# A decoder layer on one core: the context's projection of the cross attention in three passes instead of a plain float32 matmul

## What is computed

```python
def _L0_xattn_ref(input1, input2, ...):          # input1 = layernorm(x), input2 = ctx_2048
    theta_x = einsum('ld,bdt->btl', theta_w, input2) + theta_b
    phi_x = einsum('ld,bdt->blt', phi_w, input1) + phi_b[:, None]
    scores = einsum('btl,bls->bts', theta_x, phi_x)
    p = softmax(scores, axis=-1)
    g_x = einsum('ld,bdt->btl', g_w, input1) + g_b
    t_x = einsum('bts,bsl->blt', p, g_x)
    h = relu((t_x - mu) * rsqrt(var + LN_EPS) * ln_gamma + ln_beta)   # mu, var over all of t_x of a batch
    w_t = einsum('ol,blt->bot', out_w, h) + out_b[None, :, None]
    return w_t + input2
```

## Time and profile before

| | |
|---|---|
| time, median of 3 runs | 2928.14 us (2927.73 to 2932.61) |
| profiled execution | 2930.81 us, its span 2929.1 us |
| mean granted TensorE clock | 0.982 |
| PE busy | 2793.4 us, 95% |
| DVE busy | 1236.7 us, 42% |
| ACT busy | 877.9 us, 30% |
| Pool busy | 838.8 us, 29% |

### The profile page before, as it was taken

One profiled execution on the slowest core, in us unless ns is written; L12 is line 12 of the kernel. 1 busy time (PEld: TensorE's weight loads), 2 busy tenths in 40 slices (PEclk: granted clock), 3 DMA queues, 4 the chain that ended last, 5 costly groups with the idle time before them and its releaser, 6 DMA issues.

```text
span 2929.1 us, 45881 instructions
## 1 busy us (share of the span) xinstructions
PE 2793.4 (95%) x16150; PEld 2283.9 (78%) x16150; DVE 1236.7 (42%) x2152; ACT 877.9 (30%) x1697; POOL 838.8 (29%) x1306
## 2 busy tenths in 40 slices
PE   6989999988999939999999999999999999999998
PEld 6865555556666529999999999999999999999997
DVE  6756777747888833332232232132133133133111
ACT  1126666641555512221121121122122122122110
POOL 4546776631166641101101111011021021011010
PEclk9999999999999969999999999999999999999999
DMA  3101222242122223221122032032033033022010
GB/s 109 43 1 31 48 45 48 55 92 87 68 84 75 77 83 106 91 86 64 51 92 75 26 108 83 15 109 87 12 108 101 11 100 104 14 90 85 26 47 21
DMA packets 97078, 194.68 MB, mean 66 GB/s; under 512 B 22126, under 2 KB 23758, under 8 KB 96800
## 3 DMA queue, kind: packets, MB, share of 16 engines
q1 hardware_dynamic: 75072, 131.77, 15.1%
q0 software_dynamic: 21856, 60.73, 6.6%
HBM read 148.77 MB, written 38.94 MB: 64 GB/s over the span
## 4 chain that ended last, share of the span: by engine, by line
PE 62%; DMA 0%; POOL 0%; DVE 0%; issue 0%; ACT 0%; DVEq 0%; POOLq 0%
PE ex_hid L1775 31%; PE ex_acc L102 10%; PE ex_acc L103 10%; PE ex_acc L104 10%; PE ex_xb L1745 1%; DMA ex_ys<-xn_dram,ex_slot_gather 0%; POOL out_dram L1627 0%; POOL ex_ys L1607 0%; DVE ex_ys L1688 0%; POOL ex_xg L1592 0%; DMA ex_ys<-slot_table_dram 0%; PE ex_acc L1745 0%; DVE ex_h0l L1696 0%; ACT ex_h0h L1655 0%; DVE ex_xT0l L1671 0%
## 5 line engine op out<-in xcount | busy, mean ns | idle before, releaser
L1696 DVE SCALAR_TENSOR_TENSOR ex_h0l<-ex_hid,ex_h0h 128x640 fp32r<-128x640 f32 x128 | 105.5, 824 | 682.8 <-ACT ex_h0h L1655 682.8
L1696 DVE SCALAR_TENSOR_TENSOR ex_h1l<-ex_hid,ex_h1h 128x640 fp32r<-128x640 f32 x128 | 105.4, 824 | 602.9 <-ACT ex_h1h L1655 602.3
L1655 ACT ACTIVATE ex_h0h<-ex_hid 128x640 fp32r<-128x640 f32 x128 | 90.1, 704 | 734.5 <-PE ex_hid L1775 734.5
L1655 ACT ACTIVATE ex_h1h<-ex_hid 128x640 fp32r<-128x640 f32 x128 | 90.1, 704 | 729.8 <-PE ex_hid L1775 729.8
L654 DVE TENSOR_REDUCE at_nb<-at_ring 128x2 f32<-128x512 f32 (+1 forms) x384 | 246.8, 685 | 121.1 <-PE at_ring L760 120.9
L1597 POOL COPY ex_gi<-ex_slot_gather 128x1 int32 (+1 forms) x82 | 15.3, 187 | 918.2 <-PE ex_xb L1745 913.3
L102 PE MATMUL ex_acc<-ex_w_h,ex_h1h 128*128 128x512 f32 x640 | 254.8, 398 | 0.0
L102 PE MATMUL ex_acc<-ex_w_h,ex_h0h 128*128 128x512 f32 x640 | 253.4, 396 | 0.0
L103 PE MATMUL ex_acc<-ex_w_l,ex_h0h 128*128 128x512 f32 x640 | 250.3, 391 | 0.0
L103 PE MATMUL ex_acc<-ex_w_l,ex_h1h 128*128 128x512 f32 x640 | 250.2, 391 | 0.0
L104 PE MATMUL ex_acc<-ex_w_h,ex_h1l 128*128 128x512 f32 x640 | 249.8, 390 | 0.0
(11 more groups left out here) (273 smaller groups left out, 5665.2 us busy)
## 6 DMA issues: line engine op xcount, KB each, us to landing
ex_raw<-in_w_tiles_dram SPq DMA_DIRECT2D x256, 256.0 KB, 2.8
x_in<-in_x_dram SPq DMA_DIRECT2D x32, 256.0 KB, 2.7
act<-at_raw SPq DMA_DIRECT2D x128, 64.0 KB
at_recb<-o_rec_dram SPq DMA_DIRECT2D x16, 512.0 KB
k<-in_x_dram SPq DMA_DIRECT2D x32, 256.0 KB, 2.7
cx_ctx<-in_ctx_dram SPq DMA_DIRECT2D x16, 512.0 KB, 3.8
out_dram<-cx_res SPq DMA_DIRECT2D x16, 512.0 KB, 2.8
xn_dram<-cx_prob SPq DMA_DIRECT2D x16, 512.0 KB, 2.8
```

The costliest lines, as they stand in the source:

```text
L1655: act.activation(h[f % 2][0][:], hid[:, :, 0:HB], ACT.Relu).then_inc(sm["h_hi"], 1)
L1696: dve.scalar_tensor_tensor(h[f % 2][1][:], hid[:, :, 0:HB], 0.0, f32(h[f % 2][0][:]), ALU.max, ALU.subtract).then_inc(sm["h_lo"], 1)
```

## The change

`theta` is done in three passes as `phi` and `g` are. `theta_w` joins the weights that are split at the head of the kernel into a rounded part and a remainder. The context gets a float32r pair as well: `ctx_hi`, rounded by ACT at the end of the step two ahead of its batch (`context_hi`, behind `xin_hi`), and `ctx_lo`, the remainder, by Pool at the head of the step before its batch (`context_lo`, ahead of `group_root`). PE's `theta` waits for `ctx_lo` instead of the load, SP's reload waits for `ctx_lo` instead of `theta`. The room for the new tiles comes from `pT`, of which there is one instead of two.

```diff
-        pT = [s.sb(f"cx_pT{c}", [P, NTT, D]) for c in range(CB)]
+        ctx_hi = [s.sb(f"cx_ctxh{c}", [P, TPB, D], F32R) for c in range(CB)]
+        ctx_lo = [s.sb(f"cx_ctxl{c}", [P, TPB, D], F32R) for c in range(CB)]
+        pT = [s.sb("cx_pT", [P, NTT, D])] * CB
...
                     wait(sp, sm["ctx_res"], n + 1)
-                    wait(sp, sm["theta"], n + 1)
+                    wait(sp, sm["ctx_lo"], n + 1)
                     load(n + 2, a, j)
...
+            def context_lo(n, c):
+                wait_apart(pool, sm["ctx_hi"], n + 1, sm["passed_pool"])
+                pool.tensor_tensor(ctx_lo[c][:], ctx_in[c][:], f32(ctx_hi[c][:]), ALU.subtract)\
+                    .then_inc(sm["ctx_lo"], 1)
+
             def step(j, n, a):
                 routed = within(j - 1, 0, groups - 1)
+                if within(n + 1, 0, B):
+                    context_lo(n + 1, 1 - a)
                 if within(n - 1, 0, B):
                     group_root(n - 1, 1 - a)
...
+            context_lo(0, 0)
             steps(pool, step)
...
+            def context_hi(n, c, i):
+                act.wait_ge(ctx_loaded[c], ONE + 16 * i + 16)
+                wait(act, sm["theta"], n + 1 - CB)
+                act.activation(ctx_hi[c][:], ctx_in[c][:], ACT.Copy).then_inc(sm["ctx_hi"], 1)
...
                     xin_hi(n + 2, a)
+                    context_hi(n + 2, a, j + 2 - a)
 
             for c in range(CB):
                 xin_hi(c, c)
+            context_hi(0, 0, 0)
+            context_hi(1, 1, 0)
...
             def theta(n, c, i):
-                pe.wait_ge(ctx_loaded[c], ONE + 16 * i + 16)
+                pe.wait_ge(sm["ctx_lo"], ONE + n + 1)
                 pe.wait_ge(sm["gT_kept"], ONE + n + 1)
                 for k in range(TPB):
-                    m = pe.matmul(bank[c][2][:], t["theta_w"][:, k, :], ctx_in[c][:, k, :],
-                                  start=k == 0, stop=k == TPB - 1)
+                    m = split_passes(pe, bank[c][2][:], [w[:, k, :] for w in t["theta_w"]],
+                                     (ctx_hi[c][:, k, :], ctx_lo[c][:, k, :]), k == 0, k == TPB - 1)
                 m.then_inc(sm["theta"], 1)
...
-            split = ("phi_w", "g_w")
+            split = ("phi_w", "g_w", "theta_w")
```

More of the change, by code:

```diff
@@ L919, in stage_cross @@
         stored = [s.sem(f"cx_stored{c}") for c in range(CB)]
-        names = ("xin", "ctx_res", "xin_hi", "xin_lo", "theta", "phi", "g", "theta_hi", "theta_lo",
+        names = ("xin", "ctx_res", "ctx_hi", "ctx_lo", "xin_hi", "xin_lo", "theta", "phi", "g", "theta_hi", "theta_lo",
                  "phi_hi", "phi_lo", "gT_kept", "gT_turned", "g_kept", "scores", "neg_max", "exp", "rinv", "norm", "turned",
```

## The result

The changed kernel takes 2951.88 us (median of 6 runs, 2949.02 to 2952.93), the kernel before in the same comparison 2931.32 us (6 runs, 2927.73 to 2932.81): a ratio of 1.0072, 95% interval 1.0062 to 1.0082, +20.6 us. The forecast was 2946 us (+17.7), range 2937 to 2958, slower with 0.87. The sign holds and the time lies within the range, but three terms or links of the sum don't hold, and a part of the agreement is luck: two errors lie in opposite directions.

What follows compares the result with a forecast made beforehand. PE, DVE and Pool were taken to be within a microsecond of each other. Even steps 6.0, odd steps 11.5, steps 1 and 2 -0.4, heads 0.3 and 0.3 sum to +17.7 us: 2946 us, range 2937 to 2958.

Steps and rivals of the forecast that it cites:

- Where the time is: In the cross-attention stage, the added subtraction costs through Pool's queue and the port shared with DVE.
- ACT's copy, SP's wait and the single `pT`: At the step's end ACT's 1.08 us copy fits its idle time; SP's wait and one `pT` cost nothing.
- The projection: On PE, three passes take 1.50 us instead of 1.72, saving 0.22 us a projection, at most 3.5 us.
- Even step: Steps 4, 6 to 14: DVE's products stand behind Pool's subtraction; +1.2 less 0.22, +1.0 a step, 6.0 us.
- Odd step: Steps 5, 7 to 13: the subtraction behind the scatters delays `grstd`, `scaled`, `hid` and `xn3`; +2.3 a step, 11.5 us.
- the next link: In odd steps, later maxima push residual and `exsum`, which starts `route_rank`; `xn3` moves from 879.42 to 881.7.
- Steps 1 to 3: Steps 1 and 2 have nothing else on Pool, -0.2 us each; step 3 waits for DVE or Pool, 0.
- Queue only: DVE's products slip past Pool, so even steps add +0.1 on PE; +12.3 us in all, 2940.5; chance 0.13.
- Hidden: Pool's remainder is covered and `group_root` comes in time; -2.7 us, 2925.4; chance 0.13.
- The clock: Longer PE gaps bring the lower clock level in every step; +11 us on top, 2957; chance 0.17.
- The stage of the constants and the prologue: Two weight-splitting copies on DVE, +0.3 us; batch 0's remainder late for the first projection, +0.5 less 0.2.
- lower bound: Even-step lock costing 0 and odd steps 2.0 us, given as 2940 us.

Runs made afterwards that it cites:

- e1: Changed kernel with Pool's subtraction cut to 8 of 512 columns per row tile, the remainder zero elsewhere; 2930.10 us, 0.9992 of the kernel before.
- e2: As e1, but with the full subtraction in the even steps 4 to 14; 2933.42 us, 1.0008 of the kernel before.
- e8: Changed kernel with DVE's `exsum` of the odd steps moved ahead of the two late maxima; 2948.77 us, 1.0057 of the kernel before.
- e3: As e1, but with the full subtraction in the odd steps 5 to 13; 2944.49 us, 1.0044 of the kernel before.
- e6: Changed kernel with Pool's subtraction moved behind `group_root`; 2949.81 us, 1.0064 of the kernel before.
- e11: Changed kernel with Pool's subtraction replaced by a memset and a 960-column iota that only write, remainder zero; 2940.31 us, 1.0035 of the kernel before.
- e12: Changed kernel with DVE's residual of the odd steps moved behind the late normalisations; 2954.47 us, 1.0081 of the kernel before.

## Why the prediction was right, point by point

- **Where the time is**: right. All but 0.7 us of it lies in the stage, on Pool's queue and on the port, and e1 shows that the rest of the change costs nothing. ACT's copy, SP's wait and the single `pT` at nothing: right. The projection gave 0.16 to 0.34 us where 0.22 was forecast.
- **Even step**, forecast 1.2 less 0.22, measured 0.67 less 0.2: the mechanism is right (`gsq` held 2.02 us), the term too large. From the start of `gsq` to that of `place` it was 6.08 us (846.86 to 852.94, the latter in the earlier trace rows) and is 7.01, so 0.93 went on, not 1.2; step by step between e1 and e2 it is 0.60, for `place` and for PE alike. PE meets the delay first at a wait for `rt_lg`, which the prediction did not list. Over six steps the term was some 3 us too large.
- **Odd step**, forecast 2.3, measured 2.47: right in size, and right for `grstd`, `scaled`, `hid` and the output matmuls. The wait for `hid` is 1.83 us, not 2.2. Wrong was the next link, that `exsum` still starts `route_rank`: e8 refutes it, since with an early `exsum` the pair stays. From the end of `grstd` to `rt_prob` it was 3.86 us with 0.88 idle and is 3.98 with none; the scatter, pushed behind the residual, fills the gap with a second microsecond of its own. The two nearly cancel, so that this term came out right is in part luck. The turns at the ends of steps 6 and 7 are 21.47 us apart (forecast 21.3, before 18.99).
- **Steps 1 to 3**, forecast -0.4, measured +5.3: the failed step of the prediction. It said that steps 1 and 2 "have nothing else on Pool" and looked at Pool's queue alone. With Pool idle the subtraction starts as soon as ACT has rounded the context, and that is in the middle of DVE's `xn3`, on PE's path. The prediction priced the port for two-input operations at the place where it had looked, and did not ask which DVE operation the subtraction meets in the steps where Pool is free. The terms of the steps 4 to 15, 2 us too large together, hid a part of it: the +20.6 us lie 2.9 us above the forecast, where this step alone was 5.4 us off. That is luck.
- **Rivals.** Queue only: refuted by `gsq` at 2.18 us and by e2's pair. Hidden: refuted by the time, and by e3. The clock: it happens (3.02 us for four matmuls from step 9 on), and the prediction was right that `xn3`'s wait covers it in odd steps; at the head of the stage, where nothing covers it, it costs 1.6 us. The measured 2951.9 us lie just above the band that the prediction gave to its own account (2941 to 2951) and in the one it gave to this rival, but what lifted them there are the early steps, not the clock in every step.
- **The stage of the constants and the prologue**, +0.3 each: PE's first projection waited 0.21 us for the remainder, and the first turn comes 0.25 us later after the stage's entry. Right in size for the prologue; the other is too small to be seen between two executions.
- **The working itself** has two slips. Its lower bound, even steps at 0 and odd ones at 2.0, comes to 2937 to 2939 us and not to 2940; the range began at 2937 all the same. And PE alone would have reached the turn at 881.3, not 881.2, which changes nothing.

Put together, forecast against measured: the steps from 4 on 17.5 against 15.3 us (0.72 + five pairs of 2.89 + 0.15), the first three intervals -0.4 against +5.0, and for the rest +0.6 against +0.3, which is what is left of the 20.6 us.

## What to carry to other kernels

Before an operation with SBUF inputs is given to Pool, look up what DVE runs beside it in every kind of step, those where Pool is idle included: there it starts at once, and may land in the middle of DVE's critical instruction. Price Pool's time one for one where its queue has no idle time, and expect a queue that is pushed to meet other partners: here a scatter fell from 0.36 us ahead of DVE's residual to 0.11 us behind it and doubled. When an idle time in the profile ends with an operation that was ready long before in another queue, as `exsum` was, move that first; here it was worth 4.3 us, more than the change could have been, though the idle time explains only a part of these.

## What the runs showed of the hardware

- The hold by Pool covers DVE operations with two SBUF inputs down to one element (2.18 us beside Pool's subtraction, 0.16 beside a memset) as well as those of 512 (`scaled`, 2.08 us in e6, 0.75 alone) and, which I had not expected, `xn3`, an operation with one SBUF tensor and two per-partition scalars: 3.03 us for two beside the subtraction, 1.72 beside a memset, 1.00 alone. The Trainium skill, SBUF — State Buffer, "Who interferes with whom", lists `tensor_scalar` among the operations that can take the shared ports in a two-port mode; the trace agrees. The Trainium skill also says there that a two-input DVE instruction does not contend with a Pool instruction that only writes; e11's 0.16 us agrees.
- The hold by DVE stretches Pool's indirect DMAs. They take 0.96 us, 1.94 to 2.02 when they start 0.03 to 0.11 us behind DVE's 1.21 us residual, 1.51 us when they start 0.16 us behind `scaled` (0.75 us), and again 0.96 when they start only 0.05 us ahead of the residual (834.20 against 834.25 in e1). In the kernel before, the last odd step has the long form too (1.95 us at 1022.26, residual at 1022.16). The Trainium skill infers at the same place that `tensor_tensor` leaves descriptor generation alone; here the whole instruction took twice as long beside one. It also reads its offsets from SBUF tiles, and which of its parts was held is not shown.
- A gap of 1.83 us in front of PE was followed by full clock in steps 5 and 7 (four matmuls in 1.98 us) and by a stretch at the lower level from step 9 on (3.02 to 3.14 us), in the same execution. Behind the same gap the lower level came in e3 only in step 5, in e8 from step 11 on, and in e12 in no steady step. What decides it is open.
